# Two edits to a recurrent block on eight cores: the cast of the wide weights changes engine in the first chunk, and two weaves start with two units of the first list

## What is computed

```python
xn = layernorm(x)
# recurrent branch
gate = xn @ Wg.T;  u = xn @ Wi.T
y    = causal_conv4(u) + conv_b                       # per channel, 4 taps
ig   = sigmoid(y @ lru_Wi.T + lru_bi)
rg   = sigmoid(y @ lru_Wg.T + lru_bg)
alpha = exp(-8 * softplus(lam) * rg)
beta  = sqrt(1 - alpha**2 + 1e-6)
h[t]  = alpha[t] * h[t-1] + beta[t] * ig[t] * y[t]    # scan over the sequence
attn  = (gelu(gate) * h) @ Wo.T
# feed-forward branch with a token shift
xr, xk = mu * xn + (1 - mu) * shift(xn)               # two different mu
ffn   = sigmoid(xr @ W_r.T) * (relu(xk @ W_k.T)**2 @ W_v.T)
out = x + attn + ffn
```

## Time and profile before

| | us |
|---|---|
| median of 2 runs | 2005.8 (2005.53 to 2006.08) |
| the profiled execution, its own time | 2018.55 |
| span of its slowest core (core 6) | 2016.9 |
| spans of its eight cores | 1982.0 to 2016.9 |
| mean granted PE clock per core | 0.879 to 0.884 of full speed |

### The profile page before, as it was taken

How to read it: one execution, slowest core, us unless ns; L and a number is a source line. 1 busy time by engine, 2 the same in 40 slices (tenths; PEclk the granted TensorE clock), 3 DMA queues, 4 the chain that set the end, 5 groups by cost and what they waited for, 6 DMA issues and landing times.

```text
span 2016.9 us, 22560 instructions; the slowest of 8 cores (1982.0 to 2016.9 us)
## 1 busy us (share of the span) xinstructions
PE 1521.2 (75%) x6179; PEld 632.1 (31%) x6304; DVE 909.4 (45%) x1224; ACT 730.9 (36%) x1110; POOL 390.7 (19%) x556
## 2 busy tenths in 40 slices
PE   1447336468967897869967897878967896879887
PEld 0123112123423343324423342323423442334332
DVE  7540236436056442656056442656056532656025
ACT  2111341302364036433364136422364136423452
POOL 0114105030041102120042102120042103120122
PEclk7879667679979899889978998989988998989997
DMA  4659426476523663236523663236523653335442
GB/s 116 188 188 321 135 92 215 130 238 210 157 71 104 177 170 110 77 120 190 158 70 99 185 173 107 82 120 176 157 70 101 198 165 102 97 120 162 137 125 74
DMA packets 117258, 286.77 MB, mean 142 GB/s; under 512 B 13712, under 2 KB 13712, under 8 KB 117136
## 3 DMA queue, kind: packets, MB, share of 16 engines
q1 hardware_dynamic: 93456, 228.69, 39.1%
q10 hardware_dynamic: 17280, 31.46, 4.9%
q0 software_dynamic: 6400, 25.17, 3.1%
HBM read 243.33 MB, written 41.94 MB: 141 GB/s over the span
## 4 chain that ended last, share of the span: by engine, by line
PE 55%; issue 11%; DVE 11%; ACT 9%; DMA 6%; POOL 5%; ACTq 2%; DVEq 0%; POOLq 0%; SPq 0%
PE pb L291 52%; POOL xbh L494 4%; DVE igs L498 2%; DVE igs L490 2%; ACTq L582 2%; DMA ring<-lwi 1%; ACT alpha L477 1%; ACT beta L483 1%; DVE scr L525 1%; ACT beta L480 1%; PE pb L350 1%; DVE ring L270 1%; DVE scr L427 1%; POOL ring L270 1%; PE pb L354 1%
## 5 line engine op out<-in xcount | busy, mean ns | idle before, releaser
L291 PE MATMUL pb<-y_bf,ring 128*128 128x512 bf16 x2256 | 515.0, 388 | 30.4 <-POOL ring L270 25.5
L291 PE MATMUL pb<-xn_bf,ring 128*128 128x512 bf16 x1509 | 352.1, 389 | 67.2 <-DVE ring L270 43.3
L291 PEld LDWEIGHTS pb<-y_bf,ring 128*128 128x128 bf16 x2304 | 228.1, 100 | 319.5 <-issue 62.3
L490 DVE SCALAR_TENSOR_TENSOR igs<-ti_hf,beta 128x512 f32<-128x512 f16 x96 | 74.7, 778 | 455.1 <-ACT beta L486 455.0
L291 PE MATMUL pb<-ka_bf,ring 128*128 128x512 bf16 x501 | 167.4, 496 | 136.2 <-DVE scr L525 94.6
L291 PE MATMUL pb<-xk_bf,ring 128*128 128x512 bf16 x502 | 148.9, 451 | 128.6 <-ACT scr L513 71.7
L291 PEld LDWEIGHTS pb<-xn_bf,ring 128*128 128x128 bf16 x1536 | 151.3, 100 | 265.8 <-issue 94.4
L416 ACT ACTIVATE u_bf<-pb 128x512 bf16<-128x512 f32 x96 | 55.5, 600 | 436.2 <-PE pb L291 266.8
L494 POOL TENSOR_TENSOR xbh<-igs,y_bf 128x512 f32<-128x512 f32 x84 | 97.0, 1155 | 530.9 <-DVE igs L490 530.9
L498 DVE TENSOR_TENSOR_SCAN igs<-alpha,hc,xbh 128x512 f32<-128x512 f32 x96 | 123.2, 1284 | 147.3 <-POOL xbh L494 146.0
L291 PE MATMUL pb<-gg_bf,ring 128*128 128x512 bf16 x752 | 172.2, 386 | 11.8 <-POOL gg_bf L505 5.5
(11 more groups left out here) (73 smaller groups left out, 1367.2 us busy)
## 6 DMA issues: line engine op xcount, KB each, us to landing
ring<-lwi_s SPq DMA_DIRECT2D x84, 384.0 KB, 3.4
ring<-lwg_s SPq DMA_DIRECT2D x84, 384.0 KB, 3.5
ring<-wi_s SPq DMA_DIRECT2D x84, 256.0 KB, 3.7
ring<-wg_s SPq DMA_DIRECT2D x84, 256.0 KB, 2.7
ring<-wo_s SPq DMA_DIRECT2D x56, 384.0 KB, 3.3
out<-x_sb ACTq DMA_DIRECT2D x64, 256.0 KB, 3.5
x_sb<-x ACTq DMA_DIRECT2D x56, 256.0 KB, 10.1
ring<-wr_s SPq DMA_DIRECT2D x56, 256.0 KB, 3.1
```

The lines of the kernel that those rows point to most:

```text
L291: return e.matmul(p[:, :], rsv[:, kh * 128:(kh + 1) * 128], v, start=st, stop=sp)
L490: e.scalar_tensor_tensor(o, i, 1.0, b, ALU.add, ALU.mult),
```

## The change

Two independent edits. The cast of a wide weight tile in chunk 0 goes from POOL to DVE, where the narrow ones already are; its load (SP queue) and its store (POOL queue) stay where they were. And `weave` puts the first two units of its first list ahead and then alternates. It serves both weaves of every chunk, so their order becomes E_0, E_1, E_2, C2, E_3, C2, E_4, C2, E_5, C2, E_6, C2, E_7, C2: the last C2 of a weave stands behind E_7, where two E units stood behind it before. No instruction is added or taken away.

```diff
@@ fetch_weight @@
-            ceng = "gpsimd" if K == H else "vector"
-            P.op(ceng, lambda e, o=rsv, i=stage: e.tensor_copy(o, i),
+            P.op("vector", lambda e, o=rsv, i=stage: e.tensor_copy(o, i),
                  reads=[t_ring[2 * q], t_ring[2 * q + 1]], writes=[t_ring[s]])
@@ weave @@
-            out = []
+            out = list(aa[:2])
             na, nb = len(aa), len(bb)
-            i = k = 0
+            i, k = 2, 0
             while i < na or k < nb:
                 if i < na:
                     out.append(aa[i]); i += 1
```

## The result

The changed kernel is slower: 1.0284 times the time before (95% interval 1.0267 to 1.0301), about 57 us on 2005.8. Its profiled execution took 2063.2 us, with a span of 2061.6 us on the slowest core.

A forecast was written before the change was run, and what follows sets the result against it. PE was taken to set the pace in long stretches, the rest being handovers where it waits for elementwise engines. +36 (chunks 1 to 6), -2.6 (last chunk) and +18 (chunk 0) gave +51 on 2005.8: 2057 us, range 2024 to 2085.

The forecast's parts named there:

- First weave, chunks 1 to 6: The last C2, now behind all E units, ends later on ACT and delays A's start: +3.2 us per chunk.
- rival in which banks decide: What follows a weave waits for a PSUM bank, not the last C2; first weaves gain 5.4 us: 1986 us, chance 0.05.
- neutral weave: The weave costs nothing in later chunks, only chunk 0 and the last chunk count: 2019 us, chance 0.14.
- Second weave: Chunks 1 to 6: first C2 and the last `gg` slip 1.5 us, D starts slower: +2.8 us per chunk.
- clock term: D's start after PE's longer idle runs at a lower clock: up to 1.7 us lost, 1.3 taken.
- The six chunks: Chunks 1 to 6, both weaves together: 6 x (3.2 + 2.8) = +36 us (25 to 41).
- Last chunk: No A there; C1 follows the last E unit, with two C2 fewer ahead: -5.4, with +2.8 at D: -2.6 us.
- Chunk 0: Sum of the cast and weave effects in chunk 0's stages: +18 us.
- jump from A to C1: Chunk 0: first DVE cast of C1's second half queues behind the whole token shift: +14.3, cumulated +11.3 us.
- D of chunk 0: Each cast of `wo` waits behind DVE's add of the group before; 5.1 us a group taken: +9.6 us (6 to 24).
- low-clock rival: Chunk 0 stays at the lower clock, D at 7.2 us a group, second weave +5: 2078 to 2083 us, chance 0.14.
- Late stores: Rival: each DVE cast holds up a store's issue by 0.96 us, 31 us at most: 2088 us, chance 0.05.

The follow-up runs named there:

- lead_one: Kernel before with one E unit put ahead instead of two, in both weaves, wide casts on POOL: 1.0095 times the time before.
- keep_warm: Changed kernel plus 16 unread matmuls ahead of each of the last two steps of D's first group, chunks 1 to 7: 1.0233 times the time before.
- cast_only: Kernel before with only the wide casts moved to DVE, both weaves in their old order: 1.0103 times the time before.
- cast_split: Changed kernel with the 12 wide casts of C1's second half in chunk 0 back on POOL: 1.0183 times the time before.
- combo: Kernel before with nested's edit, early x casts, two E units ahead in chunk 0 and last chunk's first weave, `hc` copy on DVE, POOL's `gg` deferred: 0.9926.
- nested: Kernel before with each E unit of the second weave inside the C2 before it, between product and scan, chunks 1 to 7: 0.9923 times the time before.
- E2: Not a run: a stage of the kernel, whose units are woven with C2 in the second weave, ahead of D; no time of its own.

## Why the prediction was right

The forecast, 2057 with a range of 2024 to 2085, holds about 2063. The mechanism was right in both weaves, and so were the two places of the cast edit; the closeness of the sum is in part luck, as the last paragraph of this section says. Step by step:

- **First weave, chunks 1 to 6: +3.2, measured +3.3.** The mechanism is the one named. ACT's idle is 0.41 + 0.35 = 0.76 us (0.8 in the sum), A's first matmul 35.7 us after the first Relu (35.5), PE's wait 13.64 (10 or more). The rival in which banks decide falls: PE's groups were early and A didn't care. So does the neutral weave. lead_one confirms the size by its half, +1.7. One working doesn't hold as it is written: 8 of 23 matmuls in 5.34 us is 1.86 us, not 1.74. The 1.74 itself is near the 1.72 and 1.68 between the three Relus.
- **Second weave: +2.8, measured +3.3.** The slip was 1.5 by the stop matmul and by what keep_warm left. The clock term was mis-sized: 1.8 where I took 1.3, because I reasoned that some chunks start D at the lower clock anyway. None does: the granted clock was 1.00 in all 48 cases before. Over six chunks that is 3 us.
- **The six chunks: +36, measured +33.6.** The weaves alone gave 6 x 6.6 = 39.6; A took 0.4 more in each, and the stage B of the changed kernel was 1.3 us shorter in each (58.7 to 57.4), which the prediction didn't have. The change didn't make B shorter. The long stages B of the kernel before are those of cores 5, 6 and 7 of that one execution (59.1, 62.0 and 60.5 us on the mean of chunks 1 to 6); on cores 0 to 4 B took 57.6 us before and 57.5 after. cast_only, whose chunks 1 to 6 are those of the kernel before, has 57.4 too. There the whole chunk grew by 6.5 us, which makes +39, 3 over the sum. Timeline of the kernel before, core 6, the start of B in the chunk behind that of the earlier trace rows (whose chunk is the fourth of the eight by its times, not the fifth):

```profile
1136.61 9.06 ACTq L582 DMA_DIRECT2D x_sb<-x  x8
...
1146.68 15.54 PE L291 MATMUL pb<-xn_bf,ring 128*128 128x512 bf16 x63 [4.46 <-ACT u_bf L416]
```

ACT issues the eight loads of the next chunk's x ahead of its first eviction of u, so PE waits 4.46 us for that eviction; on core 0 of the changed kernel the loads are issued in 6.37 us, and PE waits 1.70. The last chunk has no such loads, and its B is 56.3 to 56.4 us on every core of both kernels. Why three cores were slower at it is open.
- **Last chunk: -2.6, measured -2.1.** First weave -5.8 (-5.4), second +3.7 (+2.8). C1 did follow E1_7 and not the last C2, which is why the same lead gains here what it costs elsewhere.
- **Chunk 0: +18, measured +21.9.** The jump from A to C1 was right, 14.8 against 14.3, made up of the wait behind the shift less the shift's shortening to 17.9 us; cast_split shows the place. The wait itself grew from 12.95 to 28.0 us, not to the 24 that the prediction gave as a sign: the 24 added only the 11.3 us by which C1 was to start later, not also the 3 by which A was to end sooner. Four small gains that I had counted came out smaller: -1 for the first half of C1 (+0.4), -2 for the first weave (-0.3), -1.3 for C1's second half (+0.7), -1.3 for the second weave (-0.7). C1's halves are bound by DMA, and a faster cast bought nothing there. Windows of the changed kernel over C1's first half, its second half and D (columns as in the earlier trace rows) show it: DMA share 1.00 and 0.96 in C1, and only 0.80 in D, where the casts have taken over.

```profile
173.00:217.00 44.00, 31.92 (x139) 12.93 (x141) 12.21 (x13) 8.16 (x12) 7.51 (x16) 1.00 1.00 325
340.00:382.00 42.00, 34.23 (x140) 14.12 (x141) 10.24 (x12) 8.84 (x12) 8.00 (x13) 0.93 0.96 310
448.00:485.00 37.00, 24.11 (x97) 9.66 (x100) 11.22 (x15) 0.00 (x0) 4.34 (x8) 0.95 0.80 249
```

- **D of chunk 0: +9.6, measured +6.7.** The chain of matmuls, add and cast is as named; its period is 4.56 us, the 4.6 that I had worked out for 2.4 GHz, and not the 5.1 that I took. Gaps of 1.81 us between groups didn't bring the clock down: it was granted at 0.95 over the stage, with D's slow first group (12 matmuls in 4.53 us, behind a wait of 6.25) in it. The low-clock rival falls with it.
- **The cast itself: 0.96, measured 0.958.** The last view is that of the lines by form: busy time, mean ns, idle before by releaser.

```profile
L269 DVE CAST ring<-ring 128x1536 bf16<-128x1536 f32 x32 | 30.5, 958 | 59.9 <-PE pb L290 41.7 <-DMA ring<-lwi 11.1 <-DMA lwi_s<-ring 4.0
```

- **Late stores** were more frequent than the prediction says, and cost next to nothing. On each of the eight cores the first store behind the three casts took 1.30 or 1.31 us to issue (row at 339.70). The narrow stages show it too, against the prediction's reading: on core 6 of the kernel before, the issue behind three narrow casts in a row took 0.78 us instead of 0.54. The idle ahead of the 32 wide casts that the transfer of a store ended was 0.3 to 4.1 us a core on POOL before, and is 7.2 to 17.1 us on DVE after (the row above has 4.0 of core 0's 7.2). But C1's halves grew by only 0.4 and 0.7 us, and D's chain of 4.56 us has no store in it. What share of that 1.1 us the stores have isn't shown; the 31 us of the rival are far off.

What the sum got wrong without showing it was the interaction. I treated the two edits as independent and priced the second weave of chunk 0 only for both together. There the number was right (-1.3 against -0.7), but my expectation for the order alone carried D's late start over from it and missed chunk 0 by 14 us. The total was close also because errors cancel: the small gains of chunk 0 were 5.7 too large and the clock term over six chunks 3 too small, while D in chunk 0 was 2.9 too high and the long stages B of the one execution before took 8 off the difference. That +36 met +33.6 is luck of this kind: without the stages B the six chunks cost 6 x 7.0 = 42 us on the mean of the cores.

## What to carry to other kernels

When two lists of units are woven into in-order queues, ask which list's *last* unit the next stage waits for, and put that one as early as its inputs allow; units of the other list moved ahead of it cost their whole time on the engine that both share, even if their own engine gets through them sooner. A cast that moves to a faster engine moves behind everything in that engine's queue: here 0.5 us saved a cast cost 15 us at one place, where the casts had run beside a token shift on the other engine. Price each of two edits alone as well as together, since the cover that hides one may be what the other takes away.

## What the runs showed of the hardware

- The scan on DVE, 1.27 us alone, took 2.18 us beside POOL's 128x512 product (combo). POOL pays too: its product `xbh` took 1.60 us in nested beside DVE's E2 add, and 1.16 with DVE idle; its copy of one column took 0.49 us beside a DVE instruction with two SBUF inputs, and 0.18 beside one with a PSUM input. In nested these two take up most of what a round fell short by.
- Three casts of 0.9 us each back to back on DVE held up the issue of a store on POOL: 1.31 us instead of 0.54 (row at 339.70 above), until the last cast ended. This is what the Trainium skill warns of ("SBUF — State Buffer", section "SBUF: two separate sides": a DMA issued from GpSimd can't write its descriptors while DVE copies float32 within SBUF); the trace agrees, with 0.77 us, on every core. In cast_split, with these casts on POOL, the first issue at that place took 0.58 us on every core.
- Waits of 4.74 and 4.95 us on PE were followed by a D that took 1.8 to 2.5 us longer, at a granted clock of 0.92 to 0.96 over its last 18.5 us instead of 1.00; waits of 1.8 us between the groups of chunk 0's D left the granted clock at 0.95. Unused matmuls in the wait gave the 1.8 us back, with a granted clock of 1.00.
- DMA issues on ACT's queue held up the compute instructions behind them: the eight loads of x took 9.06 us on core 6 before, and PE stood still for 4.46 us for the eviction behind them.
